# A one-core transformer tower: transposes and their PSUM copy moved forward in every second slot

## What is computed

```python
h = gelu(take(codebook, x) @ W1 + b1) @ W2 + b2            # token MLP
xn = layernorm(h)                                          # 256 columns: 128 token, 128 position
q = rotate(xn[..., 128:] @ Wq); k = xn[..., 128:] @ Wk; v = xn[..., :128] @ Wv   # 16 heads, 4 key/value heads, D = 64
att = q @ k.T / sqrt(64) + exp(log_slope)[h] * (i - j)     # causal, 512 x 512
e = exp(att - max(att)); att = e / (1 + sum(e))
h = h + (att @ v) @ Wo
p = layernorm(h) @ U1; h = h + (gelu(p @ V1 + b1) @ U2) @ V2 + b2
```

## Time and profile before

| what | value |
|---|---|
| median of 3 runs | 1066.27 us (1060.14, 1066.27, 1066.38) |
| the profiled execution | 1061.9 us |
| its span, first to last instruction | 1060.1 us |
| mean granted TensorE clock | 0.953 of full speed |
| TensorE matmuls busy | 897.4 us (85%) |
| ScalarE busy | 705.9 us (67%) |
| VectorE busy | 650.5 us (61%) |
| GpSimd busy | 630.2 us (59%) |

### The profile page before, as it was taken

How to read it: one execution, slowest core, us unless ns; L and a number is a source line. 1 busy time by engine, 2 the same in 40 slices (tenths; PEclk the granted TensorE clock), 3 DMA queues, 4 the chain that set the end, 5 groups by cost and what they waited for, 6 DMA issues and landing times.

```text
span 1060.1 us, 17067 instructions
## 1 busy us (share of the span) xinstructions
PE 897.4 (85%) x5616; PEld 689.1 (65%) x5616; DVE 650.5 (61%) x2002; ACT 705.9 (67%) x1564; POOL 630.2 (59%) x599
## 2 busy tenths in 40 slices
PE   5999268998898979898889888888989898989666
PEld 5989255767756756676657765766567666865553
DVE  4565366776747775576747584767477756674321
ACT  5332167896688667876787578856886678778603
POOL 5000267898648856686758575877488657775610
PEclk9999679999999999999999999999999999999986
DMA  9200100000000000000001000100000000000000
GB/s 255 42 21 21 40 20 1 1 18 5 1 1 21 22 0 2 20 21 2 1 1 40 1 1 1 41 1 1 1 22 20 1 2 21 1 1 1 20 0 20
DMA packets 13766, 18.89 MB, mean 18 GB/s; under 512 B 2304, under 2 KB 11680, under 8 KB 13680
## 3 DMA queue, kind: packets, MB, share of 16 engines
q1 hardware_dynamic: 11072, 10.62, 3.3%
q0 software_dynamic: 2608, 7.18, 2.6%
HBM read 11.51 MB, written 6.29 MB: 17 GB/s over the span
## 4 chain that ended last, share of the span: by engine, by line
PE 46%; DVE 16%; ACT 16%; issue 9%; POOL 2%; DMA 0%; DVEq 0%; POOLq 0%; ACTq 0%
PE ps L823 14%; PE ps L927 10%; ACT probs L590 7%; PE ps L913 7%; PE ps L903 5%; DVE probs L717 4%; PE ps L904 3%; ACT turned_sb L597 3%; PE ps L883 3%; ACT q_both L607 2%; DVE xn L706 2%; PE ps L877 2%; DVE q_both L734 2%; PE ps L831 1%; DVE o_lo L771 1%
## 5 line engine op out<-in xcount | busy, mean ns | idle before, releaser
L560 POOL TENSOR_SCALAR probs<-probs,recip 128x512 f32<-128x512 f32 (+3 forms) x512 | 545.6, 1083 | 257.4 <-DVE recip L726 257.0
L717 DVE CUSTOM_DVE_ANT_0 probs<-ps,causal,slope 128x512 f32<-128x512 f32 (+3 forms) x512 | 259.4, 548 | 81.4 <-PE ps L904 79.9
L590 ACT ACTIVATE probs<-probs,least 128x512 f32<-128x512 f32 (+3 forms) x512 | 282.3, 553 | 17.9 <-DVE least L717 12.1
L597 ACT ACTIVATE turned_sb<-ps 128x1280 f32<-128x1280 f32 x128 | 157.4, 1230 | 109.0 <-PE ps L913 109.0
L903 PE MATMUL ps<-k_hi,q_both 128*128 128x512 f32 (+3 forms) x512 | 185.9, 363 | 30.7 <-DVE least L717 29.3
L927 PE MATMUL ps<-turned_sb,v_sb 128*64 128x512 f32 (+3 forms) x1024 | 161.1, 458 | 27.5 <-ACT turned_sb L597 27.5
L913 PE MATMUL ps<-ident,probs 128*128 128x128 f32 x1280 | 168.7, 281 | 3.6 <-POOL probs L560 2.0
L927 PEld LDWEIGHTS ps<-turned_sb,v_sb 128*64 128x64 f32 x1024 | 77.8, 142 | 118.9 <-issue 103.1
L904 PE MATMUL ps<-k_lo,q_both 128*128 128x512 f32 (+3 forms) x512 | 154.2, 326 | 0.0
L913 PEld LDWEIGHTS ps<-ident,probs 128*128 128x128 f32 x1280 | 149.8, 146 | 5.5 <-POOL probs L560 3.6
L903 PEld LDWEIGHTS ps<-k_hi,q_both 128*128 128x128 f32 x512 | 98.7, 193 | 74.1 <-DVE least L717 50.0
(11 more groups left out here) (156 smaller groups left out, 1469.5 us busy)
## 6 DMA issues: line engine op xcount, KB each, us to landing
out_dram<-h SPq DMA_DIRECT2D x8, 512.0 KB, 2.9
rows<-in_L_tok_codebook_dram SPq DMA_DIRECT2D x4, 512.0 KB, 8.8
token_table<-made SPq DMA_DIRECT2D x8, 256.0 KB, 2.3
w_f<-in_L_tok_W_dram SPq DMA_DIRECT2D x2, 512.0 KB, 6.6
w_f<-in_L_tok_W_dram SPq DMA_DIRECT2D x4, 256.0 KB, 8.8
wo_f<-in_L_attn_Wo_dram POOLq DMA_DIRECT2D x1, 1024.0 KB, 9.9
wq_f<-in_L_attn_Wq_dram POOLq DMA_DIRECT2D x1, 512.0 KB, 7.5
v_f<-in_L_ffn_V_dram POOLq DMA_DIRECT2D x2, 256.0 KB, 7.3
```

The lines of the kernel that those rows point to most:

```text
L560: ins = pool.tensor_scalar(at, at, recip[:, s % P_RING, q:q + 1], None, ALU.mult)
L590: act.activation(at, at, ACT.Exp, bias=least[:, s % P_RING, q:q + 1], scale=-1.0, accum_out=sums[:, s % P_RING, q:q + 1]).then_inc(exped, 1)
L597: act.activation(turned_sb[:, s % 2, :], turn_ps, ACT.Copy).then_inc(moved, 1)
L717: dve.tensor_tensor_reduce(out=probs[:, s % P_RING, at], in0=bank(unit % 2)[:, UNIT_AT[q]:UNIT_AT[q] + P * (q + 1)], in1=causal[:, at], sc ...
```

## The change

In odd slots TensorE issues `turn(s - 2)` between first(s) and unit 2 instead of at the slot's end, and ScalarE issues `move(s - 2)` in the same slot, between its third and fourth exponential, instead of at the start of slot s + 1. Even slots keep their order. The number of instructions, their shapes and all waits stay.

```diff
@@ ScalarE @@
             for s in range(SLOTS):
-                if 1 + LAG <= s < ALL + 1 + LAG:
+                if s % 2 == 1 and 1 + LAG <= s < ALL + 1 + LAG:
                     move(s - 1 - LAG)
                 for use in first(s):
                     high(*use)
                 for m in range(NT - 1):
                     if s < ALL:
                         exps(s, m)
+                if s % 2 == 1 and LAG <= s < ALL + LAG:
+                    move(s - LAG)
                 if (s - LAG) % 2 == 0 and 2 + LAG <= s <= ALL + LAG:
                     o_part((s - 2 - LAG) // 2)
                 if s < ALL:
                     exps(s, NT - 1)
@@ TensorE @@
                     product(*use)
                 if 2 + LAG <= s < ALL + 1 + LAG and (s - LAG) % 2 == 0:
                     values(s - 2 - LAG)
+                if s % 2 == 1 and LAG <= s < ALL + LAG:
+                    turn(s - LAG)
                 if s < ALL:
                     scores(s, 2)
                 burst = ("f", s // HEADS - 1, 0) in second(s)
                 if burst and LAG <= s < ALL + LAG:
                     turn(s - LAG)
                 for use in second(s):
                     product(*use)
-                if not burst and LAG <= s < ALL + LAG:
+                if s % 2 == 0 and not burst and LAG <= s < ALL + LAG:
                     turn(s - LAG)
```

## The result

The changed kernel takes 1086.97 us (1086.12 to 1087.82, 4 runs) against 1063.2 us before (1058.58 to 1066.38, 4 runs): ratio 1.023, 95% interval 1.018 to 1.028. It is slower, by 1.8 to 2.8%. The profiled execution took 1086.12 us with a span of 1084.3, so 24.2 us more than the one before, where the prediction's sum had 29.1. The mean granted clock fell from 0.953 to 0.942.

A forecast was written before the change was run, and what follows sets the result against it. TensorE's own order was taken to bound the kernel (matmuls busy 85%). Terms 20.1 + 1 + 10.1 + 8.1 - 5.3 - 4.9 = +29.1 gave 1091.0 on 1061.9 and 1095.4 on 1066.3; forecast 1093 us, range 1077 to 1106.

The forecast's parts named there:

- Transposes held by GpSimd at position 3: Position 3, six sequences: early transposes wait for head 49's normalisation behind the gather, next slot 3.35 us late, 20.1 in all.
- The clock: After each of six position 3 stalls, one stretch of TensorE at slow clock: 1.7 us each, 10.1 in all.
- The first sequence: Position 3 there has the gather but no projection: only unit 2 and what hangs on it come later, about 1 us.
- Gaps filled: Transposes fill TensorE's waits for VectorE: position 5 gains 0.75 us, 5.3 in all; position 9 gains 0.7, 4.9 in all.
- The later fourth exponential: Light slots: exponential 4 behind the copy delays VectorE and the even slot's exponential 4, 0.45 us in 18 pairs, 8.1.
- light pairs that last as long as before: Sign named beforehand: if light pairs of slots keep their length, the term of the later exponential is wrong.
- Faster, the copy was the limit: Rival: the values' waits for the copy shrink by at most 0.5 us in 34 places, 17 in all; 1044.9 us, chance 0.04.
- The stall without the clock: Rival: same stall, but the clock holds or its slow stretch falls where TensorE isn't the limit; 1080.9 us, chance 0.25.
- No change: Rival: position 3's stall is caught up in slots 4 to 6, gains and later exponentials cancel; 1062 to 1066 us, chance 0.06.

The follow-up runs named there:

- fill_clock: The changed kernel with 28 unread matmuls ahead of TensorE's wait for GpSimd at position 3 of seven sequences: 1069.64 us, ratio 1.010.
- only3: The kernel before, with the new order only at position 3 of the seven sequences with a gather: 1085.81 us, ratio 1.023.
- skip3_pe: The changed kernel with the old order at position 3 of sequences with a gather, and ScalarE copying in its old place everywhere: 1042.48 us, ratio 0.984.
- skip3_11_15: The changed kernel with the old order at positions 3, 11 and 15 of every sequence: 1057.67 us, ratio 0.998.

## Why the prediction was right, point by point

The forecast was 1093 us, the median is 1087, and the stall that makes the loss was foreseen with its place, cause and size. That the sum came so near is in part luck: one term was too large by 7.1 us, and slow stretches that nobody forecast made up for some of it.

- **Transposes held by GpSimd at position 3.** Right in place, cause and count. Idle time 4.46 where 4.17 was forecast, and a next slot late by 3.6 (fill_clock) instead of 3.35. The difference is position 2: it became 0.48 shorter, TensorE came to the wait 0.3 sooner, and GpSimd did not; head 49 is ready 11.82 us after the start of slot 50 in both kernels. Positions 2 and 3 together gave 34.2 - 3.1 = 31.1 us in six sequences, where the two terms had 20.1 + 10.1 = 30.2.
- **The clock.** Forecast 1.7 a stall, measured 2.1 (5.75 - 3.62 in the fourth sequence). The mechanism was finer than I wrote: the clock fell already within the idle time and stayed low for 4.6 us of work, instead of one stretch after it; in only3, behind a gap of 4.15 us, it fell later. With the stalls filled, position 3 alone gave back 11.5 us of 1087, 1.1%. What the prediction took from the Trainium skill (TensorE: Matmul & The Clock Gate, Part 1) doesn't bear on this term: the page says there that the ramp penalty is below 1% of a typical kernel span, and that is the ramp at a kernel's start. These stalls lie in mid-kernel, and no run here measures the ramp at the start, so the sentence is neither borne out nor contradicted, and it was no reason to leave the term out.
- **The first sequence** was to lose 1 us at its stall; its slot 3 lost 0.63.
- **Gaps filled.** Position 5: -0.95 instead of -0.75, -5.7 over all instead of -5.3. Positions 9 and 10: -11.3 + 6.7 = -4.6 instead of -4.9, which is closer than the size deserves: instead of 0.7 each, six sequences gave 0.26 to 0.57, the eighth 1.55 and the first, not counted, 0.24. That only 0.7 of 2.0 would be left, since ScalarE's copy stands ahead of the second y copy, is what skip3_pe shows: without that copy position 10 loses 0.43 instead of 1.1.
- **The later fourth exponential: the term that was mis-sized.** "With VectorE's wait gone ScalarE's exponential 4 of the even slot starts some 0.45 late. As ScalarE is full in light slots, nothing gives it back" made 18 x 0.45 = 8.1. In slots 55 and 56 of the changed kernel VectorE's tiles, ScalarE's exponentials and the first score matmul of slot 55 are these:

```profile
512.85 0.75 DVE L719 CUSTOM_DVE_ANT_0 probs<-ps,causal,slope 128x512 f32<-128x512 f32 x1
...
515.89 0.48 DVE L719 CUSTOM_DVE_ANT_0 probs<-ps,causal,slope 128x256 f32<-128x256 f32 x1
```

```profile
511.88 0.50 ACT L590 ACTIVATE probs<-probs,least 128x256 f32<-128x256 f32 x1
...
516.41 0.51 ACT L590 ACTIVATE probs<-probs,least 128x256 f32<-128x256 f32 x1 [0.35 <-DVE least L719]
```

```profile
506.85 0.47 PE L905 MATMUL ps<-k_hi,q_both 128*128 128x512 f32 x1
```

The same score matmul and the second of these exponentials in the kernel before:

```profile
494.56 0.47 PE L903 MATMUL ps<-k_hi,q_both 128*128 128x512 f32 x1
```

```profile
503.82 0.51 ACT L590 ACTIVATE probs<-probs,least 128x256 f32<-128x256 f32 x1
```

The mechanism is there. VectorE starts 0.47 behind the end of exponential 4 (512.38), tile 1 follows at 515.89, and ScalarE now waits 0.35 for it. From slot 55's start the exponential of slot 56 comes at 516.41 - 506.85 = 9.56 instead of 503.82 - 494.56 = 9.26, so 0.30 late. But TensorE's pair of slots became 0.41 shorter, for its own wait of 0.72 for the copy was gone. ScalarE's lateness reaches TensorE through the next odd slot's transposes, which wait for the copy of the even head: 1.05 us in slot 47, where skip3_pe has 0.47 (TensorE's timelines, the changed kernel, then skip3_pe).

```profile
449.08 1.28 PE L915 MATMUL ps<-ident,probs 128*128 128x128 f32 x10 [1.05 <-ACT turned_sb L597]
```

```profile
435.65 1.28 PE L917 MATMUL ps<-ident,probs 128*128 128x128 f32 x10 [0.47 <-ACT turned_sb L601]
```

Over all slots of the changed kernel the light pairs give -2.8 (7, 8), +3.6 (11, 12), -4.0 (13, 14) and +4.1 (15, 0): +1.0 in all instead of +8.1, and positions 1 and 2 became shorter as well. So the step that was mis-sized is "nothing gives it back": TensorE's vanished wait gave it back in the pairs from 7 and 13. The prediction had named this as a sign against the term, light pairs that last as long as before. The 7.1 us are more than the whole difference between 29.1 and 24.2; slow stretches at position 6 (+3.2) went the other way.

- **The rivals.** "Faster, the copy was the limit": TensorE's wait ahead of the values fell by 17.7 us, about the 17 I had priced, but 13.4 of it came back ahead of the transposes, and the time didn't fall by it. "The stall without the clock": out, by fill_clock. "No change": out.

## What to carry to other kernels

Before a step is moved forward in an in-order stream, look up when each of its inputs is really ready in every kind of slot, not in the usual one: here the input came 4 us late in six slots of 128, because another engine has a rare duty there, and these six turned a gain of 0.8% (1.6% with TensorE's half alone) into a loss of 2%. Hoist such a step by a rule that leaves those slots out, and try the two halves of a change on two engines separately; the half that removes the largest wait may be the one that costs. When the same queue has a rare job and a regular one, the rare job can often go behind the regular one that somebody waits for, but what follows it must be followed too.

## What I had not expected

The same 2.12 us of idle time at position 6 is followed by value matmuls of 4.02 us in one kernel and 2.38 us in another, and within one kernel it differs from sequence to sequence. Differences of 1.6 to 1.8 us a slot come and go so with edits elsewhere, 6.6 us between the changed kernel and fill_clock; skip3_11_15 spread over 14 us, while skip3_pe's five runs lay within 2 us. And 28 matmuls that nobody reads, put into each of seven waits, made a kernel faster by 14 to 17 us.
